# Moving a split, a transpose and half loads in the attention phase of a retention and expert kernel

## The chip, the cores and the metric

One core of a Trainium2 chip runs the whole kernel as one program. The metric is the device time of one execution in microseconds: before the change 432.53 us, the median of 3 runs (431.97 to 433.69).

## The reference

The input x is (4, 1024, 256) in float32. A layer norm is followed by a retention attention with 16 heads of 16 channels, then by a group norm over each head, an output projection and a residual. A second layer norm feeds a shared gated network and two of eight experts for each token, chosen by the token's index alone.

```
q, k, v = x @ W_q.T, x @ W_k.T, x @ W_v.T
attn = einsum('bihd,bjhd->bhij', q, k) * decay[None] / scale
y = einsum('bhij,bjhd->bihd', attn, v)
yn = (y - mean) / sqrt(var + EPS)          # per batch and head, over time and channels
x = x + (yn * gn_weight + gn_bias) @ W_o.T
shared = silu(xf @ sw1 + sb1) * (xf @ sw3 + sb3) @ sw2 + sb2
x = x + (shared + (y_expert_0 + y_expert_1) / 2) / 2   # gelu experts on layernorm(x)
```

## The kernel before

Every operand of a product is split in two float32r parts, a high part (the value cast) and a low part (the rest), and a product is three matmuls: high by high, high by low, low by high.

Phase 1 is the attention. It works on 16 pieces of 256 tokens (PARTS), four of each of the four batches. The loop `step(h)` is written out for h = 0 to 15 on each engine; b = h // 4 is the batch and s = h % 4 the piece within it. Each engine runs its own list in order, and semaphores tie the lists together. The letters h, b and s below are these. Phase 2, the shared network and the experts, follows and is not touched.

PE's step h: `project_k(h+1)` (waits for xlo of piece h+1), `project_q(h+1)`, `state_sums(h)` (L534; waits for v_copied and kexp_copied), `from_scores(h)` (L565; waits for the four masked score tiles pm), `output` of the batch before in s = 2 and 3 (24 matmuls), `k_by_tokens(h+1)` (L499), `project_v(h+1)` (signals v_done), `from_state(h)` (L550; signals y_done), `scores(h+1)` (L520). In s = 0 it also runs two small products for the group norm, `head_means` and `head_vars`, and then `scores(h+1)` waits for `gn_ve`, since the variances lie in the bank that the scores overwrite.

DVE's step h: mask the four score tiles (L1023), `decay_k`, `decay_q`, `add_state`, `gn_spread` in s = 0, `carry_state`, `low_wo` in s = 1, `ln_sums(h+3)` (statistics and ln_ve, L972), `gn_eps` in s = 0 (y_ve, L1083, signals gn_ve), `scale_x(h+2)` (multiplies the transposed input by the row of 1/sigma, L993), two residuals in s = 2 and 3, `low_split_x(h+2)` (xlo, L997), `turn_rstd(h+3)` (L986), `low_y` (L1057), `y_sums` (L1063), `gn_affine` in s = 0. From h = 13 on, the last pieces having been normed, it norms the first batch for phase 2: `ln2_sums` and `ln2_apply` (L1181) by halves.

POOL raises the variance to the power -0.5 (`ln_power`, L1367, after ln_ve; `ln2_power`, L1436, for phase 2; `gn_power`, L1371), and takes the low part of one piece of the later weights in most steps.

ACT's step h: `spread_k` (keo), `copy_k` (kexp), `high_split_x(h+2)` (xhi, L800, after x_scaled and v_done), `high_y` (yhi, L810, after y_done), `copy_v(h+1)` (vexp, L762) and the high part of a weight piece. In h = 14 `copy_v` stands ahead of `high_y`.

From piece TURNED = 3 on, 1/sigma reaches the transposed input by way of DRAM. POOL writes it as two columns into ln_r (128 partitions x 32). DVE turns ln_r in 32x32 blocks into ln_turned, so that block q has its two rows of 32 values at partitions 32q and 32q + 1. SP stores them with four DMAs (`store_rstd`, L276) and one step later loads them as a row on all partitions (`load_rstd`, L282).

SP's queue holds all other loads and stores, in this order in a step: after sc_done some stores of x1, one 512 KB piece of the later weights (`load_ffn`, L287) in LOAD_STEPS (0 to 7 and 9), `load_rstd`; after q_done a store; after kt_done `load_xt`; after v_done `load_x`; after y_done `store_rstd` and loads of the residual.

Of the kernel before, what the change touches and what calls it, by code (L numbers as in the profile page):

```python
# [9 lines left out]
ACT = mybir.ActivationFunctionType  # L10

P = 128
# [62 lines left out]
def moe_retention(nc, xa, xt, xs, wattn, gnw, gnb, sw1, sw3, sw2, w1, w2, sb1, sb3, b1, sb2, b2, decay, masks, out):  # L75
# [5 lines left out]
    with ExitStack() as ctx:  # L81
# [30 lines left out]
        ln_r = sb("ln_r", [P, 32])  # L112
        ln_turned = sb("ln_turned", [P, 32])
        ln2_st = sb("ln2_st", [P, 4, 6])
# [143 lines left out]
        def _(sp):  # L258
# [13 lines left out]
            def store_rstd(h):  # L272
                sp.wait_ge(rstd_turned, h - TURNED + 1)
                row = rstd_dram[h].rearrange("(t n) -> t n", t=TILES)
                for q in range(0, P, 32):
                    sp.dma_start(row[:, q:q + 32], ln_turned[q:q + TILES, :]).then_inc(rstd_stored, 16)  # L276

            def load_rstd(h):
                sp.wait_ge(rstd_stored, (h - TURNED + 1) * 64)
                if h >= TURNED + 2:  # L280
                    sp.wait_ge(x_scaled, h - TURNED - 1)
                sp.dma_start(rstd_row[h % 2][:], rstd_dram[h].partition_broadcast(P)).then_inc(rstd_landed, 16)  # L282

            def load_ffn(i):
                w, at = ffn_piece(i)
                src = (sw1, sw3, w1, w1, w1, w1, sw2, w2, w2, w2, w2)[i]
                sp.dma_start(w.raw[:, at], src[:, at]).then_inc(ffn_landed[i], 16)  # L287
# [37 lines left out]
            load_x(4)  # L325
            load_ffn(0)
            load_x(5)
            load_ffn(1)

# [8 lines left out]
            def step(h):  # L338
# [7 lines left out]
                if h in LOAD_STEPS:  # L346
                    load_ffn(2 + LOAD_STEPS.index(h))
                if TURNED <= h + 2 < PARTS:
# [7 lines left out]
                if b >= 2 and s == 0:  # L356
                    store_x1(b - 2, 3)
                if h + 1 < PARTS:
                    sp.wait_ge(kt_done, h + 2)
# [9 lines left out]
                if h == 13:  # L369
                    sp.wait_ge(ln_stats, PARTS)  # L370
                    load_xl(0, 1)
                sp.wait_ge(y_done, h + 1)
                if h + 3 < PARTS:
                    store_rstd(h + 3)
                if b == 0:
                    next_xres(0, s)
# [378 lines left out]
        def _(act):  # L755
# [39 lines left out]

            def high_split_x(h):

                act.wait_ge(x_scaled, h - TURNED + 1)
                act.wait_ge(v_done, h)
                nc.scalar.activation(xhi[:], xin_t[h % 2][:], ACT.Copy).then_inc(xhi_ready, 1)  # L800

            def high_y(h):
# [23 lines left out]
            def high_ffn(i):  # L826
                w, at = ffn_piece(i)
                act.wait_ge(ffn_landed[i], 16)
                if i >= 6:
                    nc.scalar.activation(w.raw[:, at], w.raw[:, at], ACT.Copy, scale=0.5 if i == 6 else 0.25).then_inc(ffn_scaled, 1)  # L830
                    act.wait_ge(ffn_scaled, i - 5)
                nc.scalar.activation(w.hi[:, at], w.raw[:, at], ACT.Copy).then_inc(ffn_hi, 1)

            def step(h):
# [13 lines left out]
                if h + 1 < PARTS:  # L848
                    copy_k(h + 1)
                if TURNED <= h + 2 < PARTS:  # L850
                    high_split_x(h + 2)
                if h == TURNED - 2:
                    high_centred(2)

                if h + 2 == PARTS:
                    copy_v(h + 1)
                high_y(h)
                if h + 2 < PARTS:
                    copy_v(h + 1)
# [92 lines left out]
        def _(dve):  # L952
# [29 lines left out]
            def turn_rstd(h):  # L982
                dve.wait_ge(ln_rstd, h + 1)
                if h > TURNED:
                    dve.wait_ge(rstd_stored, (h - TURNED) * 64)
                nc.vector.transpose(ln_turned[:], ln_r[:]).then_inc(rstd_turned, 1)  # L986

# [6 lines left out]

            def low_split_x(h):
                dve.wait_ge(xhi_ready, h + 2)
                nc.vector.tensor_tensor(xlo[:], xin_t[h % 2][:], xhi[:].bitcast(F32), ALU.subtract).then_inc(xlo_ready, 1)  # L997
# [111 lines left out]
            def step(h):  # L1109
# [19 lines left out]
                if h + 3 < PARTS:  # L1129
                    ln_sums(h + 3)  # L1130
                elif h + 3 == PARTS:
                    ln2_sums(0, 0)
                elif h + 2 == PARTS:
                    ln2_apply(0, 0)
                    ln2_sums(0, 1)
                if h + 1 == PARTS:
# [5 lines left out]
                    return  # L1142
                if b and s == 0:
                    gn_eps(b - 1, p_bank[0])
                if TURNED <= h + 2 < PARTS:
                    scale_x(h + 2)
                if b and s >= 2:
                    for j in range(2 * (s - 2), 2 * (s - 2) + 2):
                        residual(b - 1, j, p_bank[j])
                if h + 2 == PARTS:  # L1150
                    ln2_apply(0, 1)
                if h + 2 < TURNED:
                    high_x(h + 2)
                    low_x(h + 2)
                elif h + 2 < PARTS:
                    low_split_x(h + 2)
                if h + 3 < PARTS:
                    turn_rstd(h + 3)
                low_y(h)
# [375 lines left out]
```

## Time and profile before

| | |
|---|---|
| median of 3 runs | 432.53 us |
| profiled execution | 432.53 us |
| its span in the trace | 430.7 us |
| granted TensorE clock, mean | 0.995 |
| PE / PE weight load / DVE | 421.0 / 381.7 / 335.5 us busy |
| ACT / POOL | 219.3 / 87.9 us busy |
| phase 1 | up to about 190 us of the span |

Busy time is the time in which an engine has an instruction running; the span is that of the trace's first to its last instruction, and 1.8 us of the execution's time lie around it. Engine names are PE (TensorE matmul), PEld (its weight load), DVE (VectorE), ACT (ScalarE), POOL (GpSimd) and SP (the queue for DMA issues). L997 is line 997 of the kernel before. A line of a timeline gives the start in us, the duration in us, engine, line, operation, output and inputs, shape and count, and in brackets how long the engine was idle before and what released it.

### The profile page before, as it was taken

Reading aid. Unit: us, or ns where it says so; the run is one execution under the profiler, and the core shown is the slowest. Engines: PE = TensorE matmul, PEld = TensorE weight load, DVE = VectorE, ACT = ScalarE, POOL = GpSimd, SP = SyncE. Lnnn points to the kernel's source line nnn. Section 1 sums busy time; section 2 is a strip of 40 time slices with the busy share of each in tenths; the row PEclk is TensorE's granted clock in tenths of the full one; section 3 lists DMA queues with packets and bytes.
Section 4 is the critical chain, followed back from the end, with each engine's and each line's share of the span. In section 5 each row is a group of like instructions: output and inputs, shape, how many; then the busy total and the mean of one; then the engine's idle time right before and its main releaser. Section 6 shows DMA issues by size and latency. Waiting matters only on the chain.

```text
span 430.7 us, 14522 instructions
## 1 busy us (share of the span) xinstructions
PE 421.0 (98%) x6232; PEld 381.7 (89%) x6232; DVE 335.5 (78%) x791; ACT 219.3 (51%) x420; POOL 87.9 (20%) x78
## 2 busy tenths in 40 slices
PE   7998999999999989999999999999999999999997
PEld 6997998999999979998989988899888998888996
DVE  7888788876987778987798887978879878856423
ACT  3566666465755557445247235483344834346530
POOL 2062634532335132550510000100001000000000
PEclk9999999999999998999999999999999999999999
DMA  8644443443451332316460015100142001120011
GB/s 267 198 139 138 139 138 113 115 122 121 131 170 35 107 114 69 101 54 181 162 196 2 2 49 182 63 0 1 49 152 91 0 1 49 49 97 0 2 50 49
DMA packets 18185, 39.79 MB, mean 92 GB/s; under 512 B 2864, under 2 KB 5200, under 8 KB 17616
## 3 DMA queue, kind: packets, MB, share of 16 engines
q1 hardware_dynamic: 17696, 38.31, 27.8%
q8 instruction: 44, 0.72, 0.7%
q10 hardware_dynamic: 432, 0.66, 0.5%
q14 instruction: 13, 0.11, 0.1%
HBM read 30.55 MB, written 8.41 MB: 90 GB/s over the span
## 4 chain that ended last, share of the span: by engine, by line
PE 97%; issue 1%; DVE 1%; DMA 1%; POOL 0%; ACT 0%; DVEq 0%
PE bank L428 54%; PE bank L437 13%; PE bank L520 7%; PE bank L438 7%; PE bank L550 4%; PE bank L565 4%; PE bank L534 3%; PE bank L499 2%; PE bank L583 1%; DMA xin<-xa 1%; PE bank L641 0%; PE bank L455 0%; PE bank L446 0%; DVE xlo L1305 0%; DVE ln_st L1292 0%
## 5 line engine op out<-in xcount | busy, mean ns | idle before, releaser
L428 PE MATMUL bank<-x2lo,sw_hi 128*128 128x512 f32 x128 | 50.4, 394 | 0.0
L428 PE MATMUL bank<-x2hi,sw_lo 128*128 128x512 f32 x128 | 50.1, 392 | 0.0
L428 PE MATMUL bank<-x2hi,sw_hi 128*128 128x512 f32 x128 | 50.0, 391 | 0.0
L437 PE MATMUL bank<-w_both,ehi 128*128 128x512 f32 x124 | 45.0, 396 | 0.0
L881 ACT ACTIVATE sil<-bank,s1b 128x512 f32<-128x512 f32 x32 | 22.0, 688 | 44.9 <-PE bank L428 44.9
L437 PE MATMUL bank<-sw_both,ghi 128*128 128x512 f32 x124 | 44.9, 395 | 0.0
L1193 DVE STREAM_TRANSPOSE x2t<-xl 32x256 f32<-32x256 f32 x96 | 41.8, 436 | 1.8
L762 ACT ACTIVATE kexp<-bank 64x256 f32<-64x256 f32 x64 | 24.3, 379 | 31.2 <-PE bank L499 30.6
L1023 DVE TENSOR_TENSOR pm<-bank,msk 128x512 f32<-128x512 f32 x64 | 39.6, 679 | 0.0
L428 PE MATMUL bank<-xhi,wqkv_hi 128*128 128x256 f32 x128 | 37.9, 296 | 0.2 <-DVE xlo L1305 0.2
L900 ACT ACTIVATE ehi<-xres 128x512 fp32r<-128x512 f32 x32 | 20.3, 633 | 33.0 <-PE bank L438 32.5
L894 ACT ACTIVATE xres<-bank,r1b 128x256 f32<-128x256 f32 x64 | 26.8, 469 | 19.4 <-PE bank L428 19.4
L428 PE MATMUL bank<-x2hi,w_lo 128*128 128x256 f32 x128 | 36.2, 283 | 0.0
L428 PE MATMUL bank<-x2lo,w_hi 128*128 128x256 f32 x128 | 36.2, 283 | 0.0
L428 PE MATMUL bank<-x2hi,w_hi 128*128 128x256 f32 x128 | 36.2, 283 | 0.0
L428 PE MATMUL bank<-xhi,wqkv_lo 128*128 128x256 f32 x128 | 36.2, 282 | 0.0
L428 PE MATMUL bank<-xlo,wqkv_hi 128*128 128x256 f32 x128 | 36.1, 282 | 0.0
L777 ACT ACTIVATE keo<-kT,msk 128x512 f32<-128x512 f32 x32 | 21.4, 715 | 27.3 <-DVE kT L1012 27.3
L438 PE MATMUL bank<-w_both,elo 128*128 128x256 f32 x124 | 34.8, 281 | 0.0
L438 PE MATMUL bank<-sw_both,glo 128*128 128x256 f32 x124 | 34.8, 281 | 0.0
L1213 DVE SCALAR_TENSOR_TENSOR gf<-bank,s3b,sil 128x512 f32<-128x512 f32 x32 | 23.9, 748 | 13.9 <-PE bank L428 13.7
L1436 POOL TENSOR_TENSOR ln_r<-ln_ve,minus_half 128x4 f32<-128x4 f32 x8 | 8.5, 1058 | 118.9 <-DVE ln_ve L1176 118.9
(154 smaller groups left out, 1154.2 us busy)
## 6 DMA issues: line engine op xcount, KB each, us to landing
w_raw<-w SPq DMA_DIRECT2D x8, 512.0 KB, 4.2
xres<-xs SPq DMA_DIRECT2D x16, 256.0 KB, 3.6
x_scratch<-xres SPq DMA_DIRECT2D x16, 256.0 KB, 3.2
xl<-x_scratch SPq DMA_DIRECT2D x8, 512.0 KB, 4.8
xr<-x_scratch SPq DMA_DIRECT2D x4, 1024.0 KB, 4.8
xin<-xa SPq DMA_DIRECT2D x15, 256.0 KB, 3.9
out<-xr SPq DMA_DIRECT2D x7, 512.0 KB, 2.6
xin_t<-xt SPq DMA_DIRECT2D x13, 256.0 KB, 2.7
```

What stands on the lines that cost most here:

```text
L428: mm = nc.tensor.matmul(o, w[c][l], x[c][r], start=first and c == 0 and j == 0, stop=last and c == n - 1 and j == 2)
L437: nc.tensor.matmul(o.rearrange("p (k d) -> p k d", k=2), hi, w[c], start=c == 0, stop=c == n - 1, skip_group_check=True)
L438: mm = nc.tensor.matmul(o[:, 0:D], lo, w[c][:, 0, :], start=False, stop=c == n - 1, skip_group_check=True)
L520: mm = nc.tensor.matmul(p_bank[p][:, o:o + CH], keo[at, c, g, :, :], qT[h % 2][at, g, c * CH:(c + 1) * CH], start=True, stop=True)
L762: cp = nc.scalar.activation(dst[64 * h2:64 * h2 + 64, :, f, :, h2, :], src[64 * f:64 * f + 64, :, :, h2, :], ACT.Copy)
L777: cp = nc.scalar.activation(keo[:, :, :, odd, :], kT[:].rearrange("p g (c j) -> p c g j", c=CPS), ACT.Copy, scale=parity[:, odd:odd + 1])
L881: nc.scalar.activation(sil[i % 2][:], h1_bank[i % 2][:], ACT.Silu, bias=s1b[:, m:m + 1]).then_inc(sil_ready, 1)
L894: ge = nc.scalar.activation(hf[q % 2][:, m, :], e_bank[q % 4][:, m * 2 * P:(m + 1) * 2 * P], ACT.Gelu, bias=r1b[:, e, m:m + 1])
L900: nc.scalar.activation(ehi[expert_buffer(e)][:], hf[q % 2][:], ACT.Copy).then_inc(ehi_ready, 1)
L1023: nc.vector.tensor_tensor(pm[p][:], p_bank[p][:].rearrange("p (a i) -> p a i", i=CH), causal.unsqueeze(1).broadcast_to([P, CPS * GROUPS, C ...
L1193: tr = nc.vector.transpose(dst[:, :, :, i, :], src[:, :, :, j, :])
L1213: nc.vector.scalar_tensor_tensor(gf[i % 3][:], h3_bank[i % 2][:], s3b[:, m:m + 1], sil[i % 2][:], ALU.add, ALU.mult).then_inc(gf_ready, 1)
```

## The change

- `turn_rstd` transposes four 32x32 blocks, from the partitions 32q of ln_r to the columns 32q of ln_turned at partitions 0 to 31, where one instruction on 128x32 did it. The two rows of 1/sigma then lie whole at partitions 0 and 1, and `store_rstd` is one DMA.
- The cast xhi of pieces 3 to 15 goes from ACT to DVE, just ahead of the subtraction; the two are now `split_x`.
- DVE's order in a step after `ln_sums` is now: `scale_x`, `turn_rstd`, residuals, `ln2_apply`, `gn_eps`, `split_x`. `ln2_apply(0, 0)` goes from step 14 to step 13.
- ACT's `copy_v` stands behind `high_y` in h = 14 too.
- SP loads each weight piece in two halves of 256 KB, the second after q_done; `store_rstd` is issued before the wait for y_done.

```diff
-        ln_turned = sb("ln_turned", [P, 32])
+        ln_turned = sb("ln_turned", [P, P])
@@ store_rstd, load_rstd, load_ffn (SP)
-                row = rstd_dram[h].rearrange("(t n) -> t n", t=TILES)
-                for q in range(0, P, 32):
-                    sp.dma_start(row[:, q:q + 32], ln_turned[q:q + TILES, :]).then_inc(rstd_stored, 16)
+                sp.dma_start(rstd_dram[h].rearrange("(t n) -> t n", t=TILES), ln_turned[0:TILES, :]).then_inc(rstd_stored, 16)
-                sp.wait_ge(rstd_stored, (h - TURNED + 1) * 64)
+                sp.wait_ge(rstd_stored, (h - TURNED + 1) * 16)
-            def load_ffn(i):
+            def load_ffn(i, half):
                 w, at = ffn_piece(i)
+                n = (at.stop - at.start) // 2
+                at = slice(at.start + n * half, at.start + n * (half + 1))
@@ prologue (SP)
-            load_ffn(0)
+            load_ffn(0, 0)
+            load_ffn(0, 1)
             load_x(5)
-            load_ffn(1)
+            load_ffn(1, 0)
+            load_ffn(1, 1)
@@ step (SP)
                 if h in LOAD_STEPS:
-                    load_ffn(2 + LOAD_STEPS.index(h))
+                    load_ffn(2 + LOAD_STEPS.index(h), 0)
...
+                if h in LOAD_STEPS:
+                    load_ffn(2 + LOAD_STEPS.index(h), 1)
                 if h + 1 < PARTS:
                     sp.wait_ge(kt_done, h + 2)
...
-                sp.wait_ge(y_done, h + 1)
                 if h + 3 < PARTS:
                     store_rstd(h + 3)
+                sp.wait_ge(y_done, h + 1)
@@ ACT
-            def high_split_x(h):
-
-                act.wait_ge(x_scaled, h - TURNED + 1)
-                act.wait_ge(v_done, h)
-                nc.scalar.activation(xhi[:], xin_t[h % 2][:], ACT.Copy).then_inc(xhi_ready, 1)
-
-                act.wait_ge(ffn_landed[i], 16)
+                act.wait_ge(ffn_landed[i], 32)
...
-                if TURNED <= h + 2 < PARTS:
-                    high_split_x(h + 2)
                 if h == TURNED - 2:
                     high_centred(2)
-
-                if h + 2 == PARTS:
-                    copy_v(h + 1)
                 high_y(h)
-                if h + 2 < PARTS:
+                if h + 1 < PARTS:
                     copy_v(h + 1)
@@ DVE
-                    dve.wait_ge(rstd_stored, (h - TURNED) * 64)
-                nc.vector.transpose(ln_turned[:], ln_r[:]).then_inc(rstd_turned, 1)
+                    dve.wait_ge(rstd_stored, (h - TURNED) * 16)
+                for q in range(4):
+                    tr = nc.vector.transpose(ln_turned[0:32, 32 * q:32 * q + 32], ln_r[32 * q:32 * q + 32, :])
+                tr.then_inc(rstd_turned, 1)
-            def low_split_x(h):
+            def split_x(h):
+
+                dve.wait_ge(x_scaled, h - TURNED + 1)
+                dve.wait_ge(v_done, h)
+                nc.vector.tensor_copy(xhi[:], xin_t[h % 2][:]).then_inc(xhi_ready, 1)
                 dve.wait_ge(xhi_ready, h + 2)
@@ step (DVE)
                 elif h + 2 == PARTS:
-                    ln2_apply(0, 0)
                     ln2_sums(0, 1)
...
-                if b and s == 0:
-                    gn_eps(b - 1, p_bank[0])
                 if TURNED <= h + 2 < PARTS:
                     scale_x(h + 2)
+                if h + 3 < PARTS:
+                    turn_rstd(h + 3)
                 if b and s >= 2:
                     for j in range(2 * (s - 2), 2 * (s - 2) + 2):
                         residual(b - 1, j, p_bank[j])
-                if h + 2 == PARTS:
-                    ln2_apply(0, 1)
+                if h + 3 >= PARTS:
+                    ln2_apply(0, h + 3 - PARTS)
+                if b and s == 0:
+                    gn_eps(b - 1, p_bank[0])
...
                 elif h + 2 < PARTS:
-                    low_split_x(h + 2)
-                if h + 3 < PARTS:
-                    turn_rstd(h + 3)
+                    split_x(h + 2)
```

## Rows read from the trace of the kernel before

**Rows 1.** The page's first part: busy us, share of the span, instructions.

```profile
PE 421.0 (98%) x6232; PEld 381.7 (89%) x6232; DVE 335.5 (78%) x791; ACT 219.3 (51%) x420; POOL 87.9 (20%) x78
```

**Rows 2.** Waits of PE: line, releaser, us in total, times, longest.

```profile
PE bank L565 <- issue: 3.4, 2, 1.7
```

**Rows 3.** Busy time, steps 0 to 14: stretch, length, each engine.

```profile
15.00:187.00 172.00, 167.64 (x4492) 158.24 (x4490) 141.10 (x366) 103.95 (x209) 66.33 (x52) 0.99 0.40 119
```

**Rows 4.** DVE's groups by form, 0 to 190: busy us, mean ns, idle.

```profile
L997 DVE TENSOR_TENSOR xlo<-xin_t,xhi 128x512 fp32r<-128x512 f32 x13 | 9.0, 692 | 18.0 <-ACT xhi L800 18.0
...
L1181 DVE TENSOR_SCALAR xl<-xl,ln_mv,ln_r 128x256 f32<-128x256 f32 x8 | 2.8, 406 | 0.0
...
L986 DVE STREAM_TRANSPOSE ln_turned<-ln_r 128x32 f32<-128x32 f32 x13 | 2.7, 204 | 0.0
...
L1003 DVE CAST xhi<-bank 128x512 fp32r<-128x512 f32 x2 | 1.4, 690 | 1.1 <-PE bank L428 1.1
```

**Rows 5.** Timeline of DVE in phase 2, one run of transposes.

```profile
236.31 2.23 DVE L1193 STREAM_TRANSPOSE x2t<-xl 32x256 f32<-32x256 f32 x5
```

**Rows 6.** Timeline of step 3, and PE's first matmul of step 4.

```profile
54.49 1.10 POOL L1367 TENSOR_TENSOR ln_r<-ln_ve,minus_half 128x2 f32<-128x2 f32 x1 [1.51 <-DVE ln_ve L972]
...
57.10 0.69 DVE L1057 TENSOR_TENSOR ylo<-bank,yhi 128x512 fp32r<-128x512 f32 x1
...
58.28 0.38 PE L428 MATMUL bank<-xhi,wqkv_hi 128*128 128x256 f32 x1
```

**Rows 7.** Timeline of step 4; L520 is the first of the scores.

```profile
65.13 0.15 DVE L1083 TENSOR_SCALAR y_ve<-bank 128x2 f32<-128x2 f32 x1
...
65.30 1.13 POOL L1367 TENSOR_TENSOR ln_r<-ln_ve,minus_half 128x2 f32<-128x2 f32 x1 [5.79 <-DVE ln_ve L972]
...
66.39 0.34 PE L520 MATMUL bank<-qT,keo 32*128 32x64 f32 x4
...
67.31 0.65 DVE L1057 TENSOR_TENSOR ylo<-bank,yhi 128x512 fp32r<-128x512 f32 x1
```

**Rows 8.** Timeline of step 5, and PE's first matmul of step 6.

```profile
76.07 1.08 POOL L1367 TENSOR_TENSOR ln_r<-ln_ve,minus_half 128x2 f32<-128x2 f32 x1 [4.04 <-DVE ln_ve L972]
...
79.53 0.38 PE L428 MATMUL bank<-xhi,wqkv_hi 128*128 128x256 f32 x1
```

**Rows 9.** Timeline of step 8.

```profile
112.26 1.14 POOL L1367 TENSOR_TENSOR ln_r<-ln_ve,minus_half 128x2 f32<-128x2 f32 x1 [5.79 <-DVE ln_ve L972]
...
113.34 0.43 PE L520 MATMUL bank<-qT,keo 32*128 32x64 f32 x5
```

**Rows 10.** Timeline of step 9, and PE's first matmul of step 10.

```profile
122.72 1.08 POOL L1367 TENSOR_TENSOR ln_r<-ln_ve,minus_half 128x2 f32<-128x2 f32 x1 [3.70 <-DVE ln_ve L972]
...
126.06 0.38 PE L428 MATMUL bank<-xhi,wqkv_hi 128*128 128x256 f32 x1
```

**Rows 11.** Timeline of step 13, and PE's first matmul of step 14.

```profile
173.25 1.39 POOL L1436 TENSOR_TENSOR ln_r<-ln_ve,minus_half 128x4 f32<-128x4 f32 x1 [4.75 <-DVE ln_ve L1176]
...
175.94 0.38 PE L428 MATMUL bank<-xhi,wqkv_hi 128*128 128x256 f32 x1
```

**Rows 12.** Timeline of step 14's end, and PE's first matmuls of step 15.

```profile
186.00 1.55 ACT L762 ACTIVATE vexp<-bank 64x256 f32<-64x256 f32 x4
...
186.77 2.01 PE L520 MATMUL bank<-qT,keo 32*128 32x64 f32 x64
...
187.57 0.60 ACT L810 ACTIVATE yhi<-bank 128x512 fp32r<-128x512 f32 x1
...
188.72 0.91 PE L534 MATMUL bank<-vexp,kexp 128*32 128x64 f32 x64
```

**Rows 13.** Busy time in step 12 after the issue gap; 0.50 is the clock.

```profile
160.30:163.70 3.40, 3.40 (x71) 3.01 (x69) 0.88 (x3) 1.96 (x5) 0.62 (x1) 0.50 0.22 77
```

**Rows 14.** Timeline of SP in step 2.

```profile
37.03 0.43 SPq L287 DMA_DIRECT2D w_raw<-w  x1
```

**Rows 15.** Timeline of POOL in step 7.

```profile
98.23 0.70 POOL L1367 TENSOR_TENSOR ln_r<-ln_ve,minus_half 128x2 f32<-128x2 f32 x1 [4.77 <-DVE ln_ve L972]
```

## The prediction

> **What bounds the kernel now.** I read the page's busy shares first, then the waits of PE, then busy time by stretch, then DVE's groups by form, and last the timelines of single steps. The shares show PE at 421.0 of 430.7 us [rows 1]: there is little idle time to win back, and any new wait of PE adds to the end one for one. PE's own waits are 3.4 us at L565 put down to "issue", in two gaps; no wait there is for data in the steps [rows 2]. So neither ACT's cast, nor SP's queue, nor a landing sets the end today. In the sixteen steps DVE is busy 141.1 of 172.0 us, the second busiest engine [rows 3], and a step waits for it often: xlo, the last thing that `project_k` of the next step needs, stands after 18.0 us of DVE idleness in 13 steps [rows 4]. That idleness is the cover for whatever is put on DVE. The question is how much of it is left in each kind of step.
>
> **The change part by part.**
>
> *The cast xhi goes from ACT to DVE.* ACT is not on the path, so what it is spared is worth nothing. On DVE it costs one 128x512 instruction in 13 steps. Every SBUF or PSUM row of 512 columns takes 0.69 there (the cast of steps 0 to 1 from PSUM 690 ns, the subtraction 692 ns) [rows 4]. No row shows a one-source copy from SBUF to SBUF of 512 columns; the nearest is the one-source `ln2_apply` form, 406 ns for 256 columns, which is 0.41 for half the width and not half of that [rows 4]. So I take 0.73 from its start to the start of xlo, signal included. Bounds: 0.46 (if 512 columns cost what those 256 do) to 0.73. In steps whose v_done comes late (s = 2, 3) it stands exactly where ACT's stood and costs nothing.
>
> The Trainium skill ("VectorE: DVE Perf Modes", section "The perf-mode tier table") says an fp32 copy within SBUF runs at twice the rate of a two-source operation, and says the same of `tensor_scalar`. The `ln2_apply` row, 406 ns for 256 columns, doesn't show that for `tensor_scalar`; for a copy no run here shows it. By the rule the sum below would be about 4.3 us in place of 5.4.
>
> *The transpose: one instruction becomes four, and moves ahead of the split.* One took 204 ns [rows 4]. The four read different partition ranges, as the x2t transposes do (32x256 each): five of those take 2.23 us, 0.446 each, with no overlap [rows 5]. So 4 x 0.21 = 0.84; bound from below 0.41, if they overlapped as small same-place instructions do. More weighty is where they stand. `turn_rstd` waits for POOL's `ln_power`, which starts only after `ln_ve` and takes 1.08 to 1.14 us. Before, the split hid that wait; now scale_x (0.6) alone does, and the split, `gn_eps`, `low_y` and the sums queue behind it on DVE.
>
> *Step 3* (a short one): POOL ends at 54.49 + 1.10 = 55.59 [rows 6]. With 0.05 for a signal (my allowance), the transposes run 55.64 to 56.48, xhi to 57.21, xlo starts there and low_y 0.60 later at 57.81, against 57.10: DVE enters step 4 0.71 late. PE gets xlo at 57.90, before step 4 opens at 58.28, so PE doesn't wait yet.
>
> *Step 4* (s = 0): `gn_eps` is now behind the transposes, and `scores(5)` on PE waits for it, with all of PE's program queued behind. POOL ends at 65.30 + 1.13 + 0.71 = 67.14; transposes to 68.03; y_ve 0.15 to 68.18; PE can start scores at 68.23. It started at 66.39 [rows 7]. **Stall 1.84.** xhi starts at 68.10, xlo 68.83, low_y 69.43 against 67.31: DVE is 2.12 late, 0.28 more than PE.
>
> *Step 5*: POOL 76.07 + 1.08 + 2.12 = 79.27; transposes to 80.16; xhi and xlo 0.73 + 0.69 and the signal: 81.62. PE wanted 79.53 + 1.84 = 81.37 [rows 8]. **Stall 0.25.** Steps 6 and 7 have 3 us more PE work (output) and let DVE catch up: in them v_done, not DVE, releases the split.
>
> *Step 8*, as step 4 but with DVE on time: 112.26 + 1.14 = 113.40, transposes 113.45 to 114.29, y_ve to 114.44, PE 114.49 against 113.34 [rows 9]. **Stall 1.15.** DVE goes on 0.28 later than PE, as in step 4: 1.43.
>
> *Step 9*: POOL 122.72 + 1.08 + 1.43 = 125.23, transposes to 126.12, xlo there at 127.58; PE wanted 126.06 + 1.15 = 127.21 [rows 10]. **Stall 0.37.** *Step 12* costs nothing: an issue gap holds PE there anyway.
>
> *Step 13*: `ln2_apply(0, 0)` moves here from step 14, ahead of the split, and waits for POOL's `ln2_power`: 173.25 + 1.39 = 174.64 [rows 11]. Its four instructions take 1.3 (2.8 for eight is 1.4 for four, of which the next overlaps 0.1 [rows 4]) and end at 175.98; then 1.46 for the split: 177.44. PE opened step 14 at 175.94. **Stall 1.50.** What step 14 is spared is worth nothing, since DVE has room there.
>
> *Step 14, ACT's order*: `copy_v(15)` now follows `high_y`, which waits for y_done, about 0.2 after scores start at 186.77. yhi starts at 186.95, the four copies at 187.44, and they end at 187.44 + 1.55 = 188.99 plus the signal. PE's state sums started at 188.72 [rows 12]. **Stall 0.31.**
>
> *SP*: three issues fewer per step, `store_rstd` ahead of the y_done wait, weight loads cut into halves with the second half past `q_done`. `load_rstd` has half as much ahead of it, and so may land sooner. But DVE hardly waits for a landing, every weight piece is used one step or more later, and no PE wait goes back to SP. I count 0, with the halves bounded both ways by the issue gaps (rivals below). The two extra issues in the prologue come after everything that the first steps need.
>
> **Sum**: 1.84 + 0.25 + 1.15 + 0.37 + 1.50 + 0.31 = 5.42. The profiled execution took 432.53 us (span 430.7 and 1.8 around it), which is also the median shown: 432.53 + 5.4 = **437.9 us**. Lower end of the mechanism: cheap cast (0.46) and overlapped transposes (0.41) leave steps 4 and 8 at 0.70 and 0.72, step 13 at 1.23, step 14 at 0.31, 5 and 9 at none: 3.0, 435.5 us. Its largest parts are POOL's 1.1 us and ln2's 1.3, both measured, so it can't go to zero.
>
> **Rivals.**
>
> *A, the clock falls behind the new stalls (slower still).* After the issue gap of step 12, PE ran 3.40 us at a granted clock of 0.50, 1.2 GHz [rows 13]. That lost at most 1.7 us, half of 3.4. The new stalls of steps 4 (1.84) and 13 (1.50) are as long as that gap. For it: their length. Against: the other issue gap, 1.7 too, had no such stretch behind it. If both do it: 5.4 + 2 x 1.7 = 8.8, 441.3 us; one: 439.6.
>
> *B, not slower: the issue gaps go.* In them PE has its data and no instruction. One lies in step 2, a few microseconds after the step's 512 KB weight load was issued at 37.03 [rows 14]. If the instruction fetch stood behind such a load, half loads and fewer store packets free it: the gaps (3.4) and the half-clock stretch (1.7) would go, 5.1 in all, and 5.4 - 5.1 leaves 432.8 us. It decides from the point where the fetch is no longer behind a load. Against it: the second gap, in step 12, follows no weight load (LOAD_STEPS ends at 9), and the second halves are now issued at `q_done`, just before the stretch of smallest matmuls (L534, L565), where instructions are used up fastest. That could as well make a gap more: +1.7, 439.6.
>
> *C, the moved transpose isn't late.* If POOL's power is done when scale_x is (in step 7 the same instruction took 0.70 [rows 15]), steps 4 and 8 lose 0.4 each, 5 and 9 their 0.6 and step 4 the 0.3 more that step 3 hands on: 5.4 - 0.8 - 0.6 - 0.3 = 3.7, 436.2 us. Against it: 1.08 to 1.14 in all five steps that count here.
>
> *D, the change does nothing on DVE,* since the 18.0 us of idleness take 13 x 0.6 = 7.8 with room to spare. That holds for the sum of the steps, not for steps 4, 5, 8, 9 and 13, and `gn_eps` doesn't wait in that idleness but behind it. 432.5.
>
> **How the numbers follow.** Forecast 5.4 with its own spread, 436.5 to 439.3: 0.52. The low end (C, a faster cast or overlapped transposes), 435 to 436.5: 0.18. A or a new gap, 439.3 to 442: 0.15. B and D together, 431.5 to 434.5: 0.13. Something that I don't see, on either side: 0.02. Range 434.6 to 440.8, which leaves out B, D and the far end of A. About 0.5%, 2.2 us, is what a measurement here can tell from no change: from 430.4 to 434.7 counts as the same. Faster 0.03, same 0.10, slower 0.87.
>
> **What would show it.** In the changed kernel's timeline: PE idle ahead of L520 in steps 4 and 8 with DVE's y_ve as releaser (1.8 and 1.2), ahead of project_k of step 14 with xlo (1.5), small ones in steps 5 and 9; four transposes about 0.21 apart, waiting for POOL; the cast at 0.69 (0.42 would halve steps 5 and 9 and take 0.27 from 13); L534 of step 15 waiting for vexp. In PE's waits, DVE should stand with 4 to 5.5 us where the steps have none now. It would be wrong if those waits are there but the issue gaps are gone, or if y_ve is ready ahead of L520.

## The result, and the profile after

| | before | changed |
|---|---|---|
| median of 22 runs, us | 430.80 (429.79 to 436.10) | 436.38 (434.04 to 438.32) |
| the profiled execution, us (span) | 432.53 (430.7) | 434.81 (433.0) |

The changed kernel is slower: ratio 1.0104, 95% interval 1.0085 to 1.0125, 4.5 us. The two medians stand 5.6 us apart, more than the ratio gives; the ratio is of fast runs alone, and the record doesn't show what else makes the difference. The time is inside the predicted range, 1.5 us below the forecast. The profiled execution of the changed kernel took less than its median and that of the kernel before more, so the two traces show where time went, but only 2.3 us of it.

Lines moved: before's L520 is now L524, L428 L432, L565 L569, L534 L538, L762 L766, L810 L808, L1367 L1365, L1436 L1434, L997 L996, L986 L980. The page's first line, against [rows 1]:

```profile
PE 421.7 (97%) x6232; PEld 381.0 (88%) x6232; DVE 346.9 (80%) x843; ACT 211.1 (49%) x407; POOL 88.6 (20%) x78
```

PE has the same instructions and is busy 0.7 us longer. DVE has 11.4 us more, ACT 8.2 less. A data wait is idle time of PE that another engine's semaphore ends; an issue gap is idle time for which the profile shows no releaser. PE's waits in the changed kernel (us in total, times, longest), against [rows 2]:

```profile
PE bank L524 <- DVE y_ve L1082: 2.5, 3, 1.0
PE bank L711 <- DVE vexp L1287: 2.0, 1, 2.0
PE bank L432 <- DVE xlo L996: 1.6, 2, 1.4
PE bank L569 <- issue: 0.8, 1, 0.8
PE bank L554 <- issue: 0.5, 1, 0.5
...
PE bank L538 <- ACT vexp L766: 0.3, 1, 0.3
PE bank L577 <- DVE pm L1022: 0.2, 1, 0.2
```

Seven waits for data in the sixteen steps, on four lines of PE's program, stand where there were none; the seventh, 0.19 for xlo, is at the opening of step 2 (the 2.0 at L711 is of the prologue and old). The issue gaps are 1.3 here. Before they were 3.4 in the two long ones of [rows 2] and 1.0 in four short ones:

```profile
PE bank L550 <- issue: 0.4, 1, 0.4
...
PE bank L428 <- issue: 0.3, 2, 0.2
PE bank L499 <- issue: 0.3, 1, 0.3
```

DVE's groups by form, against [rows 4]:

```profile
L1179 DVE TENSOR_SCALAR xl<-xl,ln_mv,ln_r 128x256 f32<-128x256 f32 x32 | 11.0, 406 | 0.9 <-POOL ln_r L1434 0.9
L980 DVE STREAM_TRANSPOSE ln_turned<-ln_r 32x32 f32<-32x32 f32 x52 | 10.4, 200 | 7.9 <-POOL ln_r L1365 7.3
L996 DVE TENSOR_TENSOR xlo<-xin_t,xhi 128x512 fp32r<-128x512 f32 x13 | 9.0, 693 | 0.4
...
L994 DVE CAST xhi<-xin_t 128x512 fp32r<-128x512 f32 x13 | 5.5, 424 | 1.4 <-PE bank L432 1.2
```

The 18.0 us of DVE idleness ahead of xlo [rows 4] are now 7.9 ahead of the transposes, nearly all of it waiting for POOL's power, and 1.4 ahead of the cast: the in-order queue waits earlier, at the moved transpose. Step 4 in the timeline, against [rows 7] (start and duration in us; in brackets the idle time before, and what ended it):

```profile
64.91 1.08 POOL L1365 TENSOR_TENSOR ln_r<-ln_ve,minus_half 128x2 f32<-128x2 f32 x1 [5.41 <-DVE ln_ve L965]
66.03 0.84 DVE L980 STREAM_TRANSPOSE ln_turned<-ln_r 32x32 f32<-32x32 f32 x4 [0.59 <-POOL ln_r L1365]
66.80 0.10 DVE L1082 TENSOR_SCALAR y_ve<-bank 128x2 f32<-128x2 f32 x1
67.05 0.51 PE L524 MATMUL bank<-qT,keo 32*128 32x64 f32 x9 [0.83 <-DVE y_ve L1082]
```

POOL ends at 65.99, four transposes, then `gn_eps`, then PE, which had stood still for 0.83. Step 8 reads the same with a POOL power of 0.70 and a wait of 0.68, step 12 with one of 1.08 and a wait of 1.00:

```profile
160.25 0.84 DVE L980 STREAM_TRANSPOSE ln_turned<-ln_r 32x32 f32<-32x32 f32 x4 [0.58 <-POOL ln_r L1365]
161.03 0.10 DVE L1082 TENSOR_SCALAR y_ve<-bank 128x2 f32<-128x2 f32 x1
161.28 0.45 PE L524 MATMUL bank<-qT,keo 32*128 32x64 f32 x8 [1.00 <-DVE y_ve L1082]
```

Step 13 and the opening of step 14, against [rows 11], and of step 15, against [rows 12]:

```profile
171.49 1.38 POOL L1434 TENSOR_TENSOR ln_r<-ln_ve,minus_half 128x4 f32<-128x4 f32 x1 [4.50 <-DVE ln_ve L1174]
172.90 1.38 DVE L1179 TENSOR_SCALAR xl<-xl,ln_mv,ln_r 128x256 f32<-128x256 f32 x4 [0.90 <-POOL ln_r L1434]
174.20 0.42 DVE L994 CAST xhi<-xin_t 128x512 fp32r<-128x512 f32 x1
174.66 0.69 DVE L996 TENSOR_TENSOR xlo<-xin_t,xhi 128x512 fp32r<-128x512 f32 x1
175.40 0.39 PE L432 MATMUL bank<-xhi,wqkv_hi 128*128 128x256 f32 x1 [1.36 <-DVE xlo L996]
...
190.02 0.42 PE L538 MATMUL bank<-vexp,kexp 128*32 128x64 f32 x13 [0.30 <-ACT vexp L766]
```

**The account of the two profiles.** PE's data waits from step 0 on: 0.83 + 0.68 + 1.00 (y_ve), 1.36 + 0.19 (xlo), 0.30 (vexp), 0.17 (pm in step 4), 4.53 in all. Issue gaps: 0.51 (in step 0) + 0.82 (in step 2) = 1.33, in place of 4.36 in six. PE is thus idle 4.53 - 3.03 = 1.50 us more, and phase 2 opens 1.47 us later (198.25 against 196.78). The spans differ by 2.3. The other 0.8 comes in phase 2, which the change doesn't touch. Its first and last matmuls, before and then after:

```profile
196.78 0.50 PE L428 MATMUL bank<-x2hi,sw_hi 128*128 128x512 f32 x1
427.70 0.28 PE L428 MATMUL bank<-w_both,ehi 128*128 128x256 f32 x1
...
198.25 0.50 PE L432 MATMUL bank<-x2hi,sw_hi 128*128 128x512 f32 x1
429.95 0.28 PE L432 MATMUL bank<-w_both,ehi 128*128 128x256 f32 x1
```

From the one start to the other it is 230.92 us before and 231.70 after, at full clock and without a wait of PE in either. This isn't scatter: the kernel before (twice), e4, e5, e9, e10 and e11 have 230.91 or 230.92, the changed kernel, e1, e2, e3, e6, e7 and e12 have 231.69 or 231.70. The seven slower ones are those in which `ln_turned` is 128x128 and is filled by four transposes and stored at once. e5 takes back just these and has the shorter phase 2, with the cast on DVE and the new orders kept; e6, e7 and e12 take back the cast, the orders and SP's part, and have the longer one. Which of the three (the wider tile, the transposes, the store) does it, and how, no run separates. It is 0.8 us of the loss.

Each profile also has one stretch of 3.4 us at half clock: before's follows the issue gap of step 12 [rows 13], the changed kernel's follows the wait of step 13. Busy time of the latter by windows (columns as in [rows 3]; the number after POOL's is the granted clock: 1.00, then 0.50):

```profile
175.40:176.00 0.60, 0.60 (x5) 0.60 (x6) 0.60 (x2) 0.00 (x0) 0.57 (x1) 1.00 0.78 280
176.20:179.20 3.00, 3.00 (x16) 3.00 (x15) 3.00 (x7) 0.00 (x0) 3.00 (x4) 0.50 0.03 11
```

So the two profiles differ by less than the medians do, and both have one such stretch. The granted clock of every run tells how often it comes: a stretch lowers a run's mean clock by 0.004. In three sessions 45 of 93 runs of the kernel before had at least one; of the changed kernel's 39, 26 had. Within before, runs with exactly one were 2.0 to 2.5 us longer than those with none (434.12 and 431.90, 433.31 and 430.82, 433.98 and 432.00). The stretch by itself costs less. From the start of the scores in step 13 to that of the state sums in step 14 the changed kernel took 7.93 us, 1.36 of it the wait; e5, with a wait of 1.44 and no stretch, took 6.52. That leaves 1.5 us for the stretch; by what else the runs with one are longer is open.

### The profile page after: what moved, and what is told of

The parts are those of the page before. It is cut to its first block, busy times and chain, and to the rows that moved or that the text cites. A ratio compares the mean times of both kernels' runs of the same rounds, so it can differ in the third digit from the quotient of the medians.

```text
span 433.0 us, 14525 instructions
## 1 busy us (share of the span) xinstructions
PE 421.7 (97%) x6232; PEld 381.0 (88%) x6232; DVE 346.9 (80%) x843; ACT 211.1 (49%) x407; POOL 88.6 (20%) x78
## 4 chain that ended last, share of the span: by engine, by line
PE 80%; DVE 11%; issue 4%; POOL 3%; ACT 1%; DMA 1%; DVEq 0%; POOLq 0%
PE bank L432 48%; PE bank L441 13%; PE bank L442 7%; PE bank L524 4%; PE bank L554 2%; DVE pm L1022 2%; PE bank L538 2%; PE bank L569 2%; POOL ln_r L1365 1%; PE bank L503 1%; DVE ln_turned L980 1%; DVE xlo L996 1%; DVE y_st L1062 1%; DVE ln_st L955 1%; DVE ylo L1056 1%
## 5 line engine op out<-in xcount | busy, mean ns | idle before, releaser
L432 PE MATMUL bank<-x2hi,sw_hi 128*128 128x512 f32 x128 | 50.8, 396 | 0.0
L432 PE MATMUL bank<-x2hi,sw_lo 128*128 128x512 f32 x128 | 50.5, 394 | 0.0
L432 PE MATMUL bank<-x2lo,sw_hi 128*128 128x512 f32 x128 | 50.5, 394 | 0.0
L432 PE MATMUL bank<-xhi,wqkv_hi 128*128 128x256 f32 x128 | 38.7, 302 | 1.7 <-DVE xlo L996 1.6
L432 PE MATMUL bank<-xlo,wqkv_hi 128*128 128x256 f32 x128 | 36.8, 288 | 0.0
L432 PE MATMUL bank<-xhi,wqkv_lo 128*128 128x256 f32 x128 | 36.8, 288 | 0.0
L766 ACT ACTIVATE kexp<-bank 64x256 f32<-64x256 f32 x64 | 24.2, 378 | 24.8 <-PE bank L503 24.0
L432 PE MATMUL bank<-x2lo,w_hi 128*128 128x256 f32 x128 | 36.1, 282 | 0.0
L432 PE MATMUL bank<-x2hi,w_hi 128*128 128x256 f32 x128 | 36.1, 282 | 0.0
L432 PE MATMUL bank<-x2hi,w_lo 128*128 128x256 f32 x128 | 36.1, 282 | 0.0
L524 PE MATMUL bank<-qT,keo 32*128 32x64 f32 x1024 | 32.2, 273 | 2.5 <-DVE y_ve L1082 2.5
```

Source lines behind the costliest of these rows:

```text
L432: mm = nc.tensor.matmul(o, w[c][l], x[c][r], start=first and c == 0 and j == 0, stop=last and c == n - 1 and j == 2)
L524: mm = nc.tensor.matmul(p_bank[p][:, o:o + CH], keo[at, c, g, :, :], qT[h % 2][at, g, c * CH:(c + 1) * CH], start=True, stop=True)
L766: cp = nc.scalar.activation(dst[64 * h2:64 * h2 + 64, :, f, :, h2, :], src[64 * f:64 * f + 64, :, :, h2, :], ACT.Copy)
```

## The experiments

Ten different kernels (e9 is e4's program again) and a second look at the kernel before (e8), in three sessions; each ratio is to the kernel before of the same session. The kernel before wasn't the same in all: 433.45, 431.65 and 433.54 us, and 430.80 in the session of the result.

**Undoing the orders one at a time.** *e1: `gn_eps` back ahead of scale_x and the transposes.*

```
-                if b and s == 0:                 (behind ln2_apply)
-                    gn_eps(b - 1, p_bank[0])
+                if b and s == 0:                 (ahead of scale_x)
+                    gn_eps(b - 1, p_bank[0])
```

> The changed kernel with gn_eps back ahead of scale_x, nothing else. Theory 1 (DVE has lost its room in the short steps, because it idles about 0.6 us for POOL's power and then has four transposes and the cast): PE's waits for y_ve in steps 4, 8 and 12 (0.83, 0.68, 1.00, 2.5 in all) go, but xlo, which had only 0.18 and 0.13 us to spare at the ends of steps 5 and 9, becomes late there by about 0.6 each, and step 13's wait grows from 1.4 to about 2.3: PE waits fall by 0.4 only, the time is that of the changed kernel within 1 us. Theory 2 (the place of gn_eps is the cost): all 2.5 us go, nothing comes in their place, ratio to before 1.004 to 1.006.

Measured 434.86, ratio 1.0047 (1.0019 to 1.0076). PE's waits in its profile:

```profile
PE bank L432 <- DVE xlo L996: 2.4, 4, 1.4
...
PE bank L569 <- issue: 1.5, 2, 1.0
...
PE bank L538 <- ACT vexp L766: 0.3, 1, 0.3
```

y_ve is gone from the waits, xlo has gained three (0.16 in step 4, 0.41 in step 5, 0.40 in step 9). Of 2.5 us 1.0 came back as waits for xlo: between the two theories, nearer to the second.

*e2: the transposes back behind the split.*

```
-                if h + 3 < PARTS:                (behind scale_x)
-                    turn_rstd(h + 3)
+                if h + 3 < PARTS:                (behind split_x)
+                    turn_rstd(h + 3)
```

> The changed kernel with turn_rstd back behind the split, ahead of low_y; still four transposes and one store. Theory 1: DVE no longer idles for POOL ahead of y_ve and the split, so the waits for y_ve (2.5 us) go and nothing takes their place; left are step 13 (1.4) and step 15's vexp (0.3): about 1.7 to 2.5 us over before, ratio about 1.004 to 1.006. Theory 2 (four transposes and the cast are too much work for DVE wherever they stand): the waits move to xlo or pm, ratio stays near 1.010.

Measured 435.42, 1.0055 (1.0025 to 1.0084). All y_ve waits are gone; 1.8 for xlo (step 13) and 0.3 for vexp stay, and the issue gaps are back at 1.37 and 1.53. Waits and ratio are as expected. 10 of its 12 runs had a stretch at half clock.

*e3: `ln2_apply(0, 0)` back in step 14, ahead of its sums.*

> The changed kernel with ln2_apply(0, 0) back in step 14, ahead of ln2_sums(0, 1). Both theories: the wait of project_k in step 14 for xlo (1.36 us in the profile) goes. Theory 1 adds the half-clock stretch that followed this wait in the profile of the changed kernel (about 1.5 us): if the stretch comes from the wait, 1.4 to 2.9 us less than the changed kernel, ratio 1.004 to 1.008. Rival (what is spared in step 13 is paid in step 14): ratio stays 1.010, with a new wait of the scores or of state sums in step 14 or 15.

Measured 433.29, 1.0022 (0.9995 to 1.0049). The wait of 1.36 ahead of step 14 is gone; y_ve stays with 2.7. This one edit, moved by one step, is some 3.5 us by the ratios, more than its wait: 9 of 12 runs had no stretch at half clock, against 13 of 39 for the changed kernel.

*e7: all four orders of DVE and ACT as before; the cast on DVE, the four transposes and SP's part as changed.*

> The changed kernel with all four orders as before: gn_eps ahead of scale_x, turn_rstd behind the split, ln2_apply(0, 0) in step 14, copy_v ahead of high_y in step 14. Kept are the four transposes with one store, the cast on DVE, and SP's part. If the orders are all of the loss, no wait of PE for DVE or ACT stands in the steps, and the time is that of the kernel before with SP's part alone (0.995, 0.992 to 0.998). If transposes and cast (11 us more DVE work in all) cost by themselves, xlo or pm is late in the short steps and the ratio is over 1.000.

Measured 431.55, 1.0008 (0.9977 to 1.0039). PE waits for no data of a step; issue gaps 1.16 and 1.48. In the old orders the cast on DVE and the four transposes make no wait, so the waits come from the orders. Yet the ratio is 0.6% above that of SP's part alone (e4, e9 below), of which e7 differs by the cast, the transposes and the merged store. No wait in the profile answers to that. In us the distance to e9 is 1.2 (431.55 and 430.39), of which phase 2 is 0.8 (231.69 against 230.91 by the traces). The rest of the 0.6% is the divisor: in e7's session the kernel before was quicker, at full clock too (430.82 against 431.90 and 432.00). Why it was is open.

**The costs on DVE.** *e5: one transpose of 128x32 and four stores in place of four and one, at the changed place.*

```
-                for q in range(4):
-                    tr = nc.vector.transpose(ln_turned[0:32, 32 * q:32 * q + 32], ln_r[32 * q:32 * q + 32, :])
-                tr.then_inc(rstd_turned, 1)
+                nc.vector.transpose(ln_turned[:], ln_r[:]).then_inc(rstd_turned, 1)
```

> The changed kernel with one 128x32 transpose and four stores again, still at the changed kernel's place (ahead of gn_eps and the split). DVE is spared 0.84 - 0.20 = 0.64 us ahead of y_ve in each step. If the four transposes make their share of the wait, y_ve's waits fall from 0.83, 0.68 and 1.00 to about 0.2, 0 and 0.4, 1.9 us less than the changed kernel, ratio about 1.006; step 13 and vexp stay. If only POOL's power sets y_ve's time (the transposes overlap it), the waits stay at 2.5.

Measured 433.23, 1.0034 (1.0002 to 1.0066). PE in steps 4, 8 and 12, and at the opening of step 14:

```profile
66.77 2.01 PE L526 MATMUL bank<-qT,keo 32*128 32x64 f32 x64 [0.37 <-DVE y_ve L1082]
...
113.57 2.01 PE L526 MATMUL bank<-qT,keo 32*128 32x64 f32 x64 [0.38 <-DVE y_ve L1082]
...
160.23 2.01 PE L526 MATMUL bank<-qT,keo 32*128 32x64 f32 x64 [0.36 <-DVE y_ve L1082]
...
174.38 0.39 PE L434 MATMUL bank<-xhi,wqkv_hi 128*128 128x256 f32 x1 [1.44 <-DVE xlo L996]
```

0.46, 0.30 and 0.64 less than with four, where 3 x 0.21 = 0.63 is left out. In step 8 POOL's power took 1.08 here and 0.70 in the changed kernel, so that step compares two things. What is left for y_ve, 1.1 us, is more than the 0.6 that I expected. The ratio is 0.7% below the changed kernel's, some 3 us: 1.4 are the waits for y_ve, 0.8 phase 2.

*e6: the cast back on ACT.* `high_split_x(h + 2)` is again behind `copy_k`, and `split_x` only subtracts.

> The changed kernel with the cast xhi back on ACT, all orders of DVE as changed. The cast stands behind y_ve, so y_ve's waits stay (2.5 in all); only step 13's wait falls, by the cast's 0.46, to about 0.9. Time 0.5 us less than the changed kernel, ratio about 1.009. Rival (moving the cast to DVE is the costly part): waits fall by 2 us or more, ratio 1.004 or less.

Measured 435.43, 1.0078 (1.0044 to 1.0111). PE's waits:

```profile
PE bank L569 <- issue: 2.4, 2, 1.7
PE bank L524 <- DVE y_ve L1086: 2.0, 2, 1.0
...
PE bank L432 <- DVE xlo L1000: 0.8, 1, 0.8
```

The cast has no part in y_ve's waits (1.00 and 0.99), and 0.6 in step 13's (0.77 in place of 1.36). Its issue gap of 1.69 in step 12 took the place of y_ve's wait there. The ratio expected was 1.009, within the interval. Two stretches at half clock stand in this profile, one behind y_ve's wait of step 8 and one behind xlo's:

```profile
116.20:119.40 3.20, 3.20 (x15) 3.20 (x16) 2.97 (x7) 1.99 (x4) 2.72 (x2) 0.50 0.67 223
177.80:180.80 3.00, 3.00 (x16) 3.00 (x16) 3.00 (x7) 0.00 (x0) 3.00 (x3) 0.50 0.25 85
```

**SP's part.** *e4: the kernel before with SP's part alone (weight loads in halves, `store_rstd` ahead of the y_done wait).*

> The kernel before with SP's part of the change alone: weight pieces in halves, the second after q_done, and store_rstd ahead of the y_done wait (still four stores). Theory 1: nothing of it is on the path, ratio 0.998 to 1.002, no new PE wait. Rival (the issue gaps depend on the weight loads): gaps marked issue go (up to 3.4 us, ratio down to 0.992) or grow (ratio up to 1.004).

Measured 430.51, 0.9951 (0.9924 to 0.9977): faster, where I had counted 0. *e9* is the same program once more, *e10* and *e11* have one half of the edit each:

```
-                    load_ffn(2 + LOAD_STEPS.index(h))
+                    load_ffn(2 + LOAD_STEPS.index(h), 0)      (e10; the second half behind q_done)
...
-                sp.wait_ge(y_done, h + 1)
                 if h + 3 < PARTS:
                     store_rstd(h + 3)
+                sp.wait_ge(y_done, h + 1)                     (e11)
```

> The kernel before with the whole SP part (weight loads in halves, store_rstd ahead of the y_done wait), the same program as in the run of that part alone, repeated on another occasion. Theory 1 (the SP part itself is worth something, about 1.5 to 2 us): again 0.993 to 0.997 of before. Theory 2 (the first 0.9951 was the lot of one chip and hour): 0.999 to 1.001. In neither does PE wait for a data signal in the sixteen steps, so a gain must lie in the issue gaps (3.4 us in two gaps before) or in the half-clock stretches.

> The kernel before with the weight loads cut into halves alone; store_rstd stands behind y_done as before. If the instruction fetch stands behind the 512 KB loads, the halves carry the whole SP gain (ratio near that of the full SP part, the issue gap of step 2 below 1.5 us). If the stores' place or chance is what counts, 1.000 within 0.15%.

> The kernel before with store_rstd ahead of the y_done wait alone; the loads are whole. scale_x should find its row earlier by 1 to 2 us in each of 13 steps, which DVE can't use as long as PE doesn't wait for it: 1.000 by theory 'no path from SP to PE'. If this order is what gained 1.5 us in the full SP part: 0.996.

| kernel | median us | ratio (interval) | runs without a half-clock stretch | the two issue gaps, us |
|---|---|---|---|---|
| before (three sessions) | 431.65 to 433.54 | | 48 of 93 | 1.70, 1.69 |
| e9, SP's part | 430.39 | 0.9941 (0.9916 to 0.9966) | 12 of 12 | 1.17, 1.69 |
| e10, halves alone | 430.68 | 0.9949 (0.9924 to 0.9974) | 10 of 12 | 1.50, 1.42 |
| e11, store order alone | 432.52 | 1.0008 (0.9976 to 1.0040) | 7 of 12 | 1.70, 1.42 |

The halves are the whole gain as far as these runs tell. A half landed 3.5 us after its issue in e10 (2.7 to 3.5 in the ten profiles with halves), a whole piece 4.3 in e11 (3.9 to 4.6 in the four with whole loads):

```profile
w_raw<-w SPq DMA_DIRECT2D x16, 256.0 KB, 3.5
```

The gap of step 2 didn't go, it is 0.2 to 0.5 shorter. Besides the two long gaps there are short ones of 0.15 to 0.9 us. With them the issue gaps from step 0 on are 4.36, 4.85 and 4.86 us with whole loads (before, e8, e11) and 4.21, 3.45, 4.14 and 3.39 with halves (e4, e9, e10, e7), 0.9 less in the mean of a few single profiles. Two things were seen with the halves: stretches at half clock are rarer (32 of 36 runs of e4, e9 and e10 had none), worth about 2.2 x (45/93 - 4/36) = 0.8 us in the mean, and at full clock the runs are shorter too (430.57 against 432.00 in e10's session). The fewer issue gaps can be 0.9 of the second's 1.4; why half loads should make fewer of either is open. All three runs of the halves fell in sessions in which the kernel before took longer (433.45 and 433.54), so what they are worth where it takes 430.80 or 431.65 isn't shown.

*e12: the changed kernel with SP as before.*

> The changed kernel with SP as before: whole loads, store_rstd behind y_done; DVE's and ACT's changes stay. If the SP part is worth 1.5 to 2 us also under the new waits: 0.4% slower than the changed kernel, ratio to before 1.014. If it is worth nothing: 1.010 as the changed kernel. If the new waits follow from POOL's ln_power alone, PE's wait for y_ve stays at 2.5 us within 0.3 and the one for xlo at 1.6 within 0.5; were the late store of the row what makes scale_x late, xlo's wait would grow above 2.5.

Measured 437.39, 1.0126 (1.0086 to 1.0166), the slowest of all, though its interval overlaps the changed kernel's. PE's waits:

```profile
PE bank L518 <- DVE y_ve L1076: 2.2, 3, 1.0
...
PE bank L426 <- DVE xlo L990: 1.7, 2, 1.4
```

The same waits as with SP's part: they come from POOL and DVE, not from the row's store or load. In step 12 PE has an issue gap of 0.26 and then waits 0.50 for y_ve. All six of its runs had a stretch at half clock, two of them more than one.

*e8: the kernel before again, profile only.*

> The kernel before once more, for a second profile of it: if the issue gaps (1.70 and 1.69 us at L565 in steps 2 and 12) and the half-clock stretch are fixed parts of it, they stand at the same places again; if they differ from execution to execution, they explain part of the distance between single profiles, and the sum of the new waits must be compared with medians instead.

433.38, with issue gaps at the same two places:

```profile
PE bank L565 <- issue: 3.4, 2, 2.0
```

They were 1.98 and 1.39, and there the half-clock stretch came behind the first of them:

```profile
44.80:47.80 3.00, 3.00 (x50) 2.78 (x53) 0.21 (x1) 1.83 (x5) 0.00 (x0) 0.50 0.38 87
```

## Why the prediction was right, and where it wasn't

The forecast was 437.9, the measured time 436.38. In part that is luck: the sum stood on 432.53, and the kernel before took 430.80 beside the changed one. The loss is 4.5 us by the ratio and 5.6 by the medians, where 5.4 were forecast. Of the terms of the sum, those for the cast and for steps 4, 5, 8 and 9 were too high. Four things that were not in it moved the time both ways: the wait of step 12, the gains from SP's loads and fewer issue gaps, phase 2, and half-clock stretches.

**Confirmed.** The cause: DVE's new order makes PE wait. The waits stand where they were expected in steps 4, 8, 14 and 15, with the releasers named: y_ve in steps 4 and 8, xlo at the opening of step 14, vexp in step 15. With the orders taken back and all else kept (e7) none is left. PE's net idleness came through to the end of phase 1 one for one in this pair of profiles (1.50 and 1.47), less exactly in others (2.50 and 2.84 in e12 against e8, 1.41 and 0.85 in e11 against e9). DVE stands with 4.2 us in PE's waits, within the 4 to 5.5 named. Four transposes took 0.84, as taken, without overlap. Step 13 was 1.36 for 1.50, step 15 0.30 for 0.31. What ACT was spared showed nowhere. The profiles account for 2.3 us of the loss; for the rest, 2.2 us by the ratio, no trace shows where it lies.

**The cast was mis-sized.** 0.73 was taken, 0.424 + the signal is right: 0.46 from start to start (174.20 to 174.66), the lower bound. The subtraction, 512 columns with two sources, takes 693 ns. If both have the same fixed part and the copy runs at twice the rate, that part is 2 x 424 - 693 = 155 ns, and that is what a two-source instruction on two columns takes in the same trace:

```profile
62.92 0.16 DVE L1076 TENSOR_TENSOR y_dd<-y_d 128x2 f32<-128x2 f32 x1
```

The Trainium skill ("VectorE: DVE Perf Modes", section "The perf-mode tier table") was right for this copy, and the bound was the better value. For `tensor_scalar` with two per-partition operands its rule was not seen: 406 ns for 256 columns is 155 + 251, close to half of the 538 (693 - 155) that two sources need for 512.

**Steps 4 and 5, 8 and 9.** I had 1.84 + 0.25 + 1.15 + 0.37 = 3.61; measured 0.83 + 0 + 0.68 + 0 = 1.51. The first error is the cast's, handed on from step 3 into 4. The second is the price of the start: I let POOL's power begin as late as all of DVE was late (0.71 in step 4), but it follows `ln_ve`, which DVE reaches late in a step whose pace PE sets, and by then the lateness is gone. POOL started at 64.91 against 65.30 [rows 7], 0.39 earlier, and PE was 0.39 earlier there too (state sums at 61.16 against 61.55). So POOL moved with PE and not with DVE. Without the 0.71 my working gives 1.13 for step 4. PE waited 0.83, and its schedule moved by 1.05 there (from 0.39 early to 0.66 late). In step 8 POOL's power took 0.70 instead of 1.14 (rival C, there alone of the five steps). That is 0.3 of the 0.47 between the 1.15 forecast and the 0.68 measured: the wait of step 8 was 0.67 in e3 and e12, with 0.70, and 0.99 in e6, with 1.08. In steps 5 and 9 xlo was in time by less than 0.2 (in step 5 it ended at 79.61, and PE opened at 79.77). e1 shows the chain of steps that I described, 0.41 and 0.40 in just these two, when `gn_eps` doesn't let PE wait first.

**Step 12 failed as a step.** "Costs nothing: an issue gap holds PE there anyway" took a gap for a constant. In the changed kernel's profile the gap was not there, and PE waited 1.00 for y_ve in its place. The same in e3 (1.00) and e5 (0.36); in e6 the gap of 1.69 was there and no wait was seen, and in e12 there was some of each (0.26 and 0.50). As a sum this is no worse than before (1.00 for 1.69). Rival B, the issue gaps go, came true in part (1.33 for 4.36 in these two profiles), beside the waits rather than instead of them.

**Rival A was seen, and was not in the forecast.** In the profiles of the changed kernel, e1, e3, e6 and e12 a stretch of 3.4 us at half clock came with one of the new waits. By the counts it is a matter of odds: the changed kernel had one in 26 of 39 runs, e1 in 8 of 12, e2 in 10 of 12, e12 in 6 of 6, the kernel before in 45 of 93. e3 (3 of 12) and e5 (5 of 12), with waits of 1.00 and 1.44, show that the length of a wait alone doesn't decide it. A run with one is about 2.2 us longer. From 45/93 to 26/39 that adds 0.4 us in the mean, and a second stretch in a run adds to it; but so small a difference of counts can still be chance (about 6 in 100 by Fisher's exact test), so that the new waits make stretches more frequent is likely and not shown.

**SP was counted 0 and is a gain.** e4, e9 and e10 give -0.5 to -0.6%, 2.2 to 2.6 us on the kernel before; e12 against the changed kernel gives 0.9 us, within its error. The argument "no PE wait goes back to SP" was true of data waits and blind to the two things that PE loses without a semaphore: issue gaps and clock. Without SP's part (e12, 5.5 us) the change comes out near my sum, for partly other reasons: 4.1 us of waits, 0.8 in phase 2, and a half-clock stretch in each of its six runs.

**A version that beats both** is e9's: the kernel before with SP's part alone, 0.9941 of it (430.39 us) in its session; the halves alone do the same within error. Against the 430.80 us of the session of the result the margin would be small. The DVE and ACT edits gain nothing in any order tried.

## What to carry to other kernels

Where PE is busy 98% of the time, spare time of another engine is not one sum but a balance at each wait of PE: place a cross-engine round trip (here DVE to POOL and back) behind everything that PE waits for in that step, whatever the idle total says. And count losses that have no semaphore, instruction gaps and clock dips, as chances that an edit changes: take single profiles for places and mechanisms, and medians of many runs for sizes.

## What the hardware showed that I had not expected

- PE's longest issue gaps stand at the same two places, steps 2 and 12, in stretches of the smallest matmuls, but in different executions and variants the first was 0.16 to 1.98 us and the second anything from none to 1.69. Shorter ones, 0.15 to 0.9, stand at a few other places. A data wait shortly ahead or behind can take a gap's place (none in step 12 of the changed kernel, e3 and e5), share it (e12) or not (1.69 in e6).
- A stretch at 1.2 GHz lasted 3.4 us in every profile of the steps that had one. PE had been idle for 0.8 to 2.0 us shortly before. The clock fell from 0.2 us before PE was at work again (e12) to 2.2 us after (e3). The same length of idleness had none behind it elsewhere (1.69 in e9, 1.78 in e2).
- Phase 2, with the same instructions at full clock, took 230.9 us in seven profiles and 231.7 in seven others, to 0.01 us, by whether a 128x128 `ln_turned` with its four transposes and one store or a 128x32 one was in the program of phase 1.
- An fp32 copy of 128x512 within SBUF, rounding to fp32r, took 424 ns on DVE, a `tensor_scalar` of half that width 406 ns.
- POOL's power on two columns took 0.70 us in some steps and 1.07 to 1.19 in others, with the same operands and shape.
